# Fewer logit matmuls, a fifth block bank and a new order for a gated cross-attention and mixture-of-experts kernel

## What is computed

```python
# heads of 8 channels, H = 16; k = v = ctx, q = layernorm(x)
kv = jnp.einsum('bhil,bhjl->bijhl', k_, v_)
y = jnp.fft.irfft(jnp.fft.rfft(kv, n=2 * L) * jnp.fft.rfft(ssm_kernel, n=2 * L), n=2 * L)[..., :L]
out = jnp.einsum('bijhl,bhil->bjhl', y + kv * D, q_)
x = x + jnp.tanh(g_xattn[0]) * out
# z = layernorm(x); S = L = 256 wide, E = 8 experts, K = 2
probs = softmax(z @ router_w + router_b); gates = top 2 of probs, divided by their sum
expert_out = jax.nn.gelu(jnp.einsum('bsh,ehd->ebsd', z, expert_w) + expert_b[:, None, None, :])
x = x + jnp.tanh(g_ffn[0]) * (einsum('bse,ebsd->bsd', gates, expert_out) @ out_w + out_b)
```

## Time and profile before

| | us |
|---|---|
| profiled execution, device time | 115.83 |
| its span, first to last instruction | 114.0 |
| outside the span | 1.8 |
| PE matmuls busy | 103.2 |
| DVE busy | 90.2 |
| POOL busy | 63.0 |
| ACT busy | 57.2 |

### The profile page before, as it was taken

How to read it: one execution, slowest core, us unless ns; L and a number is a source line. 1 busy time by engine, 2 the same in 40 slices (tenths; PEclk the granted TensorE clock), 3 DMA queues, 4 the chain that set the end, 5 groups by cost and what they waited for, 6 DMA issues and landing times.

```text
span 114.0 us, 1919 instructions
## 1 busy us (share of the span) xinstructions
PE 103.2 (90%) x574; PEld 86.3 (76%) x574; DVE 90.2 (79%) x293; ACT 57.2 (50%) x145; POOL 63.0 (55%) x83
## 2 busy tenths in 40 slices
PE   4956999989999999996679999999999999999960
PEld 4945888868999887754568888886788888888940
DVE  0283899999999998999889969777588876866940
ACT  4074377064258718641469997465645424353300
POOL 3015799999999999999999899600000000000000
PEclk9999999999999999999999999999999999999997
DMA  2867999159872410030030000000000101111031
GB/s 79 294 165 196 297 370 324 50 180 244 227 231 87 155 35 3 0 92 0 0 95 6 0 0 0 0 0 0 0 6 0 46 11 35 46 49 46 0 98 46
DMA packets 10956, 10.02 MB, mean 88 GB/s; under 512 B 1306, under 2 KB 10946, under 8 KB 10946
## 3 DMA queue, kind: packets, MB, share of 16 engines
q1 hardware_dynamic: 9570, 8.85, 26.6%
q10 hardware_dynamic: 1376, 1.05, 2.9%
HBM read 8.82 MB, written 1.07 MB: 87 GB/s over the span
## 4 chain that ended last, share of the span: by engine, by line
PE 61%; POOL 17%; DVE 13%; ACT 4%; issue 3%; POOLq 0%; DVEq 0%
PE ring L835 11%; PE ring L837 11%; PE ring L836 11%; POOL kv_t L374 10%; PE ring L756 6%; DVE zq_t L397 4%; PE ring L757 3%; PE ring L706 3%; DVE ow_lo_t L1040 2%; POOL w_lo_t L389 2%; ACT q_t L560 2%; PE red L779 2%; POOL rstd L403 2%; PE zbank L877 2%; PE red L712 2%
## 5 line engine op out<-in xcount | busy, mean ns | idle before, releaser
L1116 DVE SCALAR_TENSOR_TENSOR mix_t<-ring,ctxT_t,mix_t 128x256 f32<-128x256 f32 x55 | 26.6, 484 | 7.8 <-ACT ring L603 6.1
L603 ACT ACTIVATE ring<-ring 128x512 f32<-128x512 f32 (+1 forms) x33 | 18.7, 568 | 20.7 <-PE ring L837 20.7
L374 POOL TENSOR_TENSOR kv_t<-ctxT_t 128x320 f32<-128x320 f32 x27 | 23.7, 908 | 8.2 <-ACT ctxT_t L515 6.5
L835 PE MATMUL ring<-w_hi_t,zT_hi_t 128*128 128x512 f32 (+1 forms) x66 | 26.1, 396 | 0.0
L837 PE MATMUL ring<-w_hi_t,zT_lo_t 128*128 128x512 f32 (+1 forms) x66 | 25.4, 385 | 0.0
L836 PE MATMUL ring<-w_lo_t,zT_hi_t 128*128 128x512 f32 (+1 forms) x66 | 25.4, 384 | 0.0
L756 PE MATMUL ring<-kv_t,toep_t 128*128 128x288 f32 x64 | 20.9, 409 | 0.2 <-DVE zq_t L1021 0.2
L757 PEld LDWEIGHTS ring<-kv_t,toep_t 128*128 128x128 f32 x64 | 12.2, 190 | 3.3
L837 PEld LDWEIGHTS ring<-w_hi_t,zT_lo_t 128*128 128x128 f32 x66 | 12.4, 188 | 2.5
L835 PEld LDWEIGHTS ring<-w_hi_t,zT_hi_t 128*128 128x128 f32 x66 | 12.5, 189 | 2.3
L836 PEld LDWEIGHTS ring<-w_lo_t,zT_hi_t 128*128 128x128 f32 x66 | 12.5, 189 | 2.1
(11 more groups left out here) (124 smaller groups left out, 170.8 us busy)
## 6 DMA issues: line engine op xcount, KB each, us to landing
ctx_t<-in_L_ffn_expert_w SPq DMA_DIRECT2D x8, 256.0 KB, 4.3
toep_t<-kpad_dram SPq DMA_DIRECT2D x3, 512.0 KB, 6.6
x_t<-in_x SPq DMA_DIRECT2D x8, 128.0 KB
out<-x_t SPq DMA_DIRECT2D x8, 128.0 KB
wlast_t<-in_L_ffn_expert_w SPq DMA_DIRECT2D x1, 768.0 KB, 7.1
ctx_t<-in_ctx ACTq DMA_DIRECT2D x2, 256.0 KB, 3.0
zq_t<-in_x ACTq DMA_DIRECT2D x2, 256.0 KB, 3.7
ctx_t<-in_ctx SPq DMA_DIRECT2D x2, 256.0 KB, 4.2
```

The costliest lines, as they stand in the source:

```text
L374: eng.tensor_tensor(dst, head.unsqueeze(1).to_broadcast([P, HB + 1, HD * CB]), windows(ctxT_t, g, h, HB + 1), ALU.mult).then_inc(done, 1)
L603: act.activation(y, y, ACT.Gelu_apprx_tanh).then_inc(gelu_ready, 1)
L835: pe.matmul(y, hi, whi, start=(c == 0), stop=False)
L1116: dve.scalar_tensor_tensor(out=acc, in0=ring[n % RING][:, L * e:L * (e + 1)], scalar=gate, in1=acc, op0=ALU.mult, op1=ALU.add).then_inc(mi ...
```

## The change

- Router weights: the high and the low part of each half lie side by side in `rw_pair`, so one matmul with 16 stationary columns gives both products with the high part of z; `route_logits` is four matmuls of 512 columns instead of six. The logits then lie in two parts on 16 partitions, and `route_rows` adds them while it transposes: four float32 matmuls against `twice` (two identities on top of each other) instead of four transposes.
- Fifth bank: block 4 goes to `obank`, which is idle then; the blocks after it use the four ring banks shifted by one.
- Loads: `last_rows` for experts 2 to 7 and the raw weights 2 and 3 are issued ahead of the x rows 0 to 3, and bias rows 2 and 3 ahead of the output bias; weights 4 no longer stand in front of bias row 3.
- Sharing out: DVE takes 7 products instead of 5 (`BY_VECTOR`), weights_low of expert 1 instead of 5, and no fold of group 0; folds of group 1 are two on DVE and two on POOL as before.
- Order: the lists of PE, ACT, DVE and POOL are written anew. On PE, `sum_channels(4)` to `(7)` come after block 4 and between blocks; on DVE, `projection_low` leaves its place ahead of `choose_values(0)`; on POOL, `relative` of experts 0 to 2 and 4 move forward.

```diff
-BY_VECTOR = (0, 5, 15, 22, 27)
-RELATIVE_BY_DVE, LOW_BY_DVE = (), (5,)
-FOLDED_BY_DVE = ((2,), (2, 3))
-FOLDED_BY_POOL = ((), (0, 1))
+BY_VECTOR = (0, 2, 5, 11, 22, 25, 27)
+RELATIVE_BY_DVE, LOW_BY_DVE = (), (1,)
+FOLDED_BY_DVE = ((), (1, 3))
+FOLDED_BY_POOL = ((), (0, 2))
+FOLDS = ((4, 0), (5, 1), (6, 2), (7, 3), (2, 0), (3, 1), (1, 0))
...
+        def block_bank(n):
+            return obank if n == RING else ring[(n - (n > RING)) % RING]
...
+            last_rows(sp, EARLY, E - EARLY)
+            for e in range(EARLY, RAW):
+                raw_weights(sp, e)
             for b in range(BG):
                 sp.dma_start(xv[:, b, :], by_channel(x, b)).then_inc(x_rows_in[b], 16)
-            last_rows(sp, EARLY, E - EARLY)
+            for e in range(EARLY, RAW):
+                raw_bias(sp, e)
...
+            pool.wait_ge(identity_ready, 1)
+            pool.tensor_tensor(twice[:, :], ident[0:2 * E, 0:E], ident[0:2 * E, E:2 * E], ALU.add).then_inc(twice_ready, 1)
...
+            def block_bank_free(n):
+                if n < RING:
+                    pe.wait_ge(read_out, 2 * H - RING + n + 1)
+                elif n == RING:
+                    pe.wait_ge(z_low_ready, BG - 1)
+                else:
+                    pe.wait_ge(mixed_in, 2 * (n - RING + (n > 2 * RING)))
...
+                both = [rw_pair[:, 2 * E * c:2 * E * (c + 1)] for c in range(C)]
+                pe.matmul(red[0][0:2 * E, :], both[0], zT_hi[:, own, 0, :], start=True, stop=False)
                 for c in range(C):
-                    for n, (w, z) in enumerate(((rw_hi, zT_hi), (rw_hi, zT_lo), (rw_lo, zT_hi))):
-                        last = pe.matmul(red[0][0:E, :], w[:, E * c:E * (c + 1)], z[:, own, c, :],
-                                         start=(c == 0 and n == 0), stop=(c == C - 1 and n == 2))
+                    pe.matmul(red[0][0:E, :], both[c][:, 0:E], zT_lo[:, own, c, :], start=False, stop=False)
+                pe.matmul(red[0][0:2 * E, :], both[1], zT_hi[:, own, 1, :], start=False,
+                          stop=True).then_inc(logits_ready, 1)
...
-                    last = pe.transpose(red[1][:, E * b:E * (b + 1)], lgT_sb[:, P * b:P * (b + 1)], ident[0:E, 0:E])
+                    last = pe.matmul(red[1][:, E * b:E * (b + 1)], lgT_sb[:, P * b:P * (b + 1)], twice[:, :],
+                                     start=True, stop=True)
...
             fold(dve, 1, 3, dve_folded)
-            projection_low()
             choose_values(0)
```

More of the change, by code:

```diff
@@ L365, in products @@
             g, h = divmod(n, H)
-            if n % H < 2:
+            if not any(by_vector(m) == by_vector(n) for m in range(H * g, n)):
                 eng.wait_ge(context_evacuated, 4 * (g + 1))
@@ L460, in _ @@
             first_inverse_std()
-            for n in range(2, 5):
+            products(pool, 3, pool_products_ready)
+            products(pool, 4, pool_products_ready)
+            for n in range(6, 11):
                 products(pool, n, pool_products_ready)
-            for n in range(6, 15):
+            for n in range(12, 15):
                 products(pool, n, pool_products_ready)
             scales(1)
-            for n in range(16, 22):
+            products(pool, 15, pool_products_ready)
@@ L467, in _ @@
+            products(pool, 16, pool_products_ready)
+            relative(pool, 0, weights_relative)
+            products(pool, 17, pool_products_ready)
+            relative(pool, 1, weights_relative)
+            router_relative_rows()
+            for n in range(18, 22):
                 products(pool, n, pool_products_ready)
+            products(pool, 23, pool_products_ready)
+            products(pool, 24, pool_products_ready)
+            relative(pool, 2, weights_relative)
             ones()
-            router_relative_rows()
@@ L481, in _ @@
-            products(pool, 31, pool_products_ready)
-            relative(pool, 2, weights_relative)
+            weights_low(pool, 2, weights_low_ready)
+            products(pool, 26, pool_products_ready)
+            products(pool, 28, pool_products_ready)
+            scales(2)
+            for n in range(29, 32):
+                products(pool, n, pool_products_ready)
             relative(pool, 3, weights_relative)
-            weights_low(pool, 2, weights_low_ready)
+            relative(pool, 4, weights_relative)
@@ L485, in _ @@
+            weights_low(pool, 3, weights_low_ready)
             fold(pool, 1, 0, pool_folded)
[L486 to L490, removed]
+            fold(pool, 1, 2, pool_folded)
+            relative(pool, 5, weights_relative)
+            relative(pool, 6, weights_relative)
+            for n in range(4, 7):
+                weights_low(pool, n, weights_low_ready)
@@ L491, in _ @@
+            relative(pool, 7, weights_relative)
             add_bias(0)
+            add_bias(1)
+            weights_low(pool, 7, weights_low_ready)
             scales(3)
-            weights_low(pool, 6, weights_low_ready)
-            weights_low(pool, 7, weights_low_ready)
-            for n in range(1, 8):
+            for n in range(2, 8):
                 add_bias(n)
@@ L775, in sum_channels @@
                     pe.wait_ge(pool_folded, sum(len(i) for i in FOLDED_BY_POOL[:g + 1]))
-                slots = [i for i in range(HD) if i < HB or i - HB not in FOLDED_BY_DVE[g] + FOLDED_BY_POOL[g]]
+                gone = [FOLDS[i][0] for i in FOLDED_BY_DVE[g] + FOLDED_BY_POOL[g]]
+                slots = [i for i in range(HD) if i not in gone]
                 for c in range(C):
@@ L914, in _ @@
             experts(3, *BLOCKS[3])
-            for n in range(4, 7):
-                sum_channels(n)
             experts(4, *BLOCKS[4])
+            sum_channels(4)
+            sum_channels(5)
+            experts(5, *BLOCKS[5])
+            sum_channels(6)
+            experts(6, *BLOCKS[6])
             sum_channels(7)
-            for n in range(5, 11):
+            for n in range(7, 13):
                 experts(n, *BLOCKS[n])
```

246 lines of the change are left out of this document (123 added, 123 removed).

## The result

The changed kernel took 114.20 us (median of four, 114.06 to 114.33) against 116.12 for the kernel before, run beside it. The ratios leave out executions more than 1.5% above the fastest of their kernel, such as the 118.51 us of the kernel before. The same kernel, timed again beside the last experiments, gave 0.9819 [0.9766, 0.9873]. The forecast was 114.3 and "within 2%" the likeliest outcome. The profiled execution took 114.24 us with a span of 112.4; forecast were 113.9 and 112.1.

What follows compares the result with a forecast made beforehand. PE's own work and its waits ahead of group 1's sums were taken as the bound. Block 5 at 57.7 plus 54.4 gave span 112.1, with 1.8 outside 113.9, on the median's footing 114.3 us; 8-in-10 range 113.2 to 116.6.

Steps and rivals of the forecast that it cites:

- case A: DVE gets the port first at group 1's folds, block 5 waits for nothing: 114.3 us on the median's footing; chance 0.48.
- The convolution stage: On PE, up to the sums of group 0: only +0.2 us, bounds 0 and +1.0.
- The step with products 2 and 5: Early on DVE: both take turns with POOL, so the first query product starts about 0.7 us later, at 14.4.
- The sums of group 0: On PE, without group 0's fold: 64 transposes instead of 56, +0.94 us.
- The blocks: Blocks 0 to 4 on PE: five times 1.37 us, with logits and rows between them, done at 55.2.
- The chains of DVE and POOL: From residual 3 at 39.5, DVE reaches group 1's folds at 49.15, POOL at 49.1; all four done at 55.8.
- The rows of logits: On PE in both routings: four transposes become eight instructions at 0.085 us, +0.34 per group, +0.7 in all.
- L1040's new place: Between accumulate 4 and 5 on DVE: costs at most 0.6 + 1.3 us, hidden by 1 us.
- Rival B: At group 1's folds POOL gets the port first; block 5 starts 2 us later, 116.2 us; chance 0.30.
- C: Turns between DVE and POOL cost less than counted, PE waits for nothing: 112.9 to 113.6 us; chance 0.14.
- D: Bias 4 lands after POOL wants it at 46.5, ahead of the folds; each us beyond costs one; chance 0.04.
- E: Shorter runs of transposes in group 0's sums lower PE's clock, slowing convolutions behind them: span up to 118; chance 0.01.

Runs made afterwards that it cites:

- e1: The changed kernel with the split of the output weights (L1040) back ahead of the choice of experts; ratio 1.0050 to the kernel before.
- e5: The changed kernel with SP's loads in the order of the kernel before; ratio 0.9895 to the kernel before.
- same_again: The changed kernel, unaltered, timed again beside the last experiments as a control; ratio 0.9819 to the kernel before.
- e9: The changed kernel with the fold of group 0 (row 2) back on DVE; ratio 0.9895 to the kernel before.
- e3: The changed kernel with the old router logits, six matmuls and four transposes per group; ratio 0.9811 to the kernel before.
- e4: The changed kernel without the fifth bank, block 4 back in a ring bank behind sums 4 and 5; ratio 0.9935 to the kernel before.
- e8: The changed kernel with four transposes of 16 rows for the logits, their parts added by one DVE instruction; ratio 0.9819 to the kernel before.
- e6: The changed kernel with one more 0.33 us DVE instruction ahead of its last z_low and first fold of group 1; ratio 0.9980 to the kernel before.
- e2: The changed kernel with one small memset on DVE ahead of its first fold of group 1; ratio 0.9892 to the kernel before.

## Why the prediction was right

The likeliest case A came, by its mechanism: MAX8 directly behind DVE's second fold, a short wait for POOL's and none ahead of block 5. That the median is within 0.1 us of 114.3 is partly luck. The span was 0.3 over the forecast, and the 0.36 by which the forecast raised the profiled execution to the median wasn't there (114.24 against 114.20); the two cancel. By its steps:

- **The convolution stage** came out near its size, though the step behind it failed. From the first convolution to sum 0 it took 14.65; before, 16.40 with two more pairs of 0.73: -0.29, forecast +0.2. But this execution is one of three (with e1 and e5) in which the granted clock was low ahead of the first convolution (0.50 to 0.57 from 9 to 12 us) and PE began late. In same_again it took 15.01 and in the other eight without the fold of e9 14.93 to 14.98, which is 0 to +0.07. The step with products 2 and 5 failed in all of them: they take 0.88 or 0.89 for two, no turn is lost, and the first query product comes 1.25 after the first convolution, as before (in the profile of the change DVE even waits 0.79 for PE in between). Product 11, for which the forecast had no lost turn, takes 0.54 in the profile of the change, where POOL was nearly done, but 0.85 to 0.90 where PE began on time. From DVE's timeline in same_again:

```profile
19.64 0.90 DVE L379 TENSOR_TENSOR kv_t<-ctxT_t 128x320 f32<-128x320 f32 x1
```

So what was forecast at the start of the stage came, in part, in its middle. That sum 0 starts at 27.53 (forecast 27.6) is chance: 0.39 later for PE, 0.5 less for the stage.
- **The sums of group 0** cost +0.63, not +0.94: the runs of 32 take 3.58 and 3.57 start to start, 0.112 for each transpose instead of 0.118. Block 0 at 46.42 (forecast 46.6).
- **The blocks** were mis-sized: blocks 0 to 3 take 5.86 start to start in the change, not four times 1.37, since those next to float32 transposes or small matmuls take 1.48 to 1.50. And the forecast's own terms add up to 55.1, not to 55.2. PE is through with block 4 at 55.7.
- **The chains of DVE and POOL** were the risky sum and held: products 25 and 27 at 3.10 for two (forecast 2.6), residual 3 at 39.37 (39.5), folds at 48.94 and 48.99 (49.15 and 49.1), all done at 55.7 (55.8), MAX8 at 53.40 (53.6), gates at 55.9 (56.4). The error of 0.5 in products 25 and 27 is covered by others that came earlier.
- **The rows of logits** were mis-sized too: eight small matmuls at 0.12, not 0.085, 0.98 in all against 0.68. In group 0 that was absorbed, together with the longer blocks: PE waits 0.16 instead of 0.6. In group 1 it is paid: 54.75 from block 5 to the end against 54.4, which is the 0.3 that the span is over the forecast. With it the logits are no gain at all (e3).
- **L1040's new place** is hidden, as forecast: it takes 61.53 to 62.8 on DVE, and PE has no wait from block 5 to 66 us. e1 prices its old one at 2.5 us.
- **Rival B** was the right one to fear. It was not decided by the sum, whose two chains stood 0.05 apart and with POOL ahead; in the trace DVE is ahead by 0.05, and by 0.05 to 0.07 in same_again, e1, e3, e4 and e8 too. e6 shows B whole: block 5 comes 1.7 us later, where the prediction wrote 1.95. That A and not B came is luck as far as the sum goes.
- **C** was true in part (no turn lost at products 2 and 5) and still brought nothing, for the turns at 25, 27 and the folds cost what they did. **D** did not come: bias 4 was issued at 39.49, no wait on POOL. **E** did not come where it was expected. The window of the first run of 32:

```profile
27.53:31.11 3.58, 3.58 (x34) 3.58 (x33) 3.58 (x11) 1.19 (x3) 3.58 (x6) 1.00 0.74 255
```

The granted clock stays at 1.00, the level of 2.4 GHz, as in the earlier trace rows, and at 1.00 in the convolutions behind it (31.11 to 34.03). It is 1.00 from the first convolution to 105 us. That it was 0.50 for some 3 us ahead of it, as told above, no rival had.

What isn't accounted for: from block 0 to the end the kernel is 2.55 us shorter (68.53 to 65.98). The waits give 2.6, the logits 0.92, the rows take 1.28; 0.3 is left over, and no row shows where.

The parts don't add up to the gain: undone one at a time they cost 2.5 (place of L1040), 1.1 (fifth bank), 0.8 (group 0's fold), 0.7 (loads) and about -0.3 (logits, within the intervals), near 5 us against 1.9. All but the logits act on the same moment, the start of block 5, and only e1 alone undoes the whole gain. The two products more on DVE and the new order of the other calls were not undone by themselves, so what they are worth is not shown.

## What to carry to other kernels

Where two engines take turns at the same memory, lay their chains side by side and ask who comes first: in e6 0.33 us more on one engine cost 1.7. Put what nobody waits for behind what sets the next choice, not ahead of it. And price a saving on the bound engine up to its next wait only: in e3 and e8 what was cut ahead of a wait came back as that wait, and only the same cut in group 1, where PE had no wait, shortened anything (54.6 and 54.3 from block 5 to the end instead of 54.75). Last, look at a second execution before a cost is read from one: product 11 took 0.54 in the profile of the change and 0.90 in its control.

## What was not expected of the hardware

- A float32 matmul on 16 rows and 8 columns stands in the trace as two instructions of 0.12 us each (0.98 for eight). Each costs as much as a transpose of 128 x 128 (0.112 to 0.118) and more than an 8-row transpose (0.085); a whole one costs three times such a transpose.
- The recorded start isn't the moment of access: with a record 0.21 us behind POOL's, DVE still had the first turn (e2); with 0.28 it had the second (e6). The Trainium skill ("SBUF — State Buffer", section "SBUF: two separate sides") gives the lock to whoever starts first; by the recorded starts e2 speaks against that, though its memset leaves a doubt.
- DVE lost no turn at products 2 and 5, and it was not for want of POOL: POOL's first product has its record at 11.57, 0.16 behind DVE's first, and yet DVE did both in 0.89 without a break. POOL waited instead: its seven products took 6.31, where three undisputed ones at 18.24 took 2.43, 0.81 each; that is 0.64 more. It is of one kind with e2: an instruction of POOL seems to ask for access later than its record starts. That is argued from these two places, not measured by itself. Another reading, that DVE keeps the turn while its next instruction is ready, fits the products but not the folds, where POOL had its turn between DVE's two (4.54 for two). At product 11 POOL was at the end of its products in the profile of the change (0.54) and in the middle of one in same_again (0.90), and at 35.23, against low parts of 1.3 us that were already running, DVE's two products took 3.10.
